# An attention output kept as hi and lo halves in DRAM, instead of split when it is read back

## What is computed

```python
x = x + attention(layernorm(x))        # 8 heads of 64; softmax(q k^T / 8) v, then @ W_out + b_out,
                                       # a layernorm with gamma, beta, (y + x_normalised) * 2**-0.5
x = x + mix(layernorm(x))              # token mixing with the previous token:
# r = sigmoid(xr @ W_r.T); k = relu(xk @ W_k.T)**2; out = r * (k @ W_v.T)
```

## Time and profile before

| what | value |
|---|---|
| median of 3 runs | 2963.3 us (2961.91 to 2963.69) |
| profiled execution, device time | 2955.59 us |
| its span, first to last instruction | 2953.8 us |
| attention pass | to about 2150 us |
| second pass | from 2154.3 us, a step each 47.6 us |
| TensorE busy | 2775.7 us (94%) |
| VectorE busy | 1795.2 us (61%) |
| ScalarE busy | 1223.7 us (41%) |
| GpSimd busy | 1342.6 us (45%) |
| mean granted TensorE clock | 0.972 of full speed |

### The profile page before, as it was taken

How to read it: one execution, slowest core, us unless ns; L and a number is a source line. 1 busy time by engine, 2 the same in 40 slices (tenths; PEclk the granted TensorE clock), 3 DMA queues, 4 the chain that set the end, 5 groups by cost and what they waited for, 6 DMA issues and landing times. The chain is left out here.

```text
span 2953.8 us, 37679 instructions
## 1 busy us (share of the span) xinstructions
PE 2775.7 (94%) x12400; PEld 1947.1 (66%) x12400; DVE 1795.2 (61%) x2888; ACT 1223.7 (41%) x1657; POOL 1342.6 (45%) x675
## 2 busy tenths in 40 slices
PE   5999999999999999999999999999959999999999
PEld 4666666566666656666665666666547777777777
DVE  5555455545645554664555456455368888888885
ACT  2334243334423432442343244233445655565554
POOL 2565355445535644563555365356613233332332
PEclk9999999999999999999999999999969999999999
DMA  3110111021111101111110111011031212111120
GB/s 100 54 26 22 52 29 26 18 55 29 26 47 27 29 22 52 31 24 50 23 33 22 48 29 29 15 29 54 22 100 58 71 57 71 60 67 67 61 71 29
DMA packets 72641, 128.39 MB, mean 43 GB/s; under 512 B 11024, under 2 KB 11536, under 8 KB 72464
## 3 DMA queue, kind: packets, MB, share of 16 engines
q1 hardware_dynamic: 72464, 126.14, 15.2%
HBM read 58.73 MB, written 33.55 MB: 31 GB/s over the span
## 5 line engine op out<-in xcount | busy, mean ns | idle before, releaser
L272 POOL TENSOR_TENSOR acc<-acc,probs 128x1024 f32<-128x1024 f32 x384 | 914.6, 2382 | 238.3 <-ACT probs L501 210.5
L354 DVE TENSOR_REDUCE half_max<-ps_max 128x1 f32<-128x512 f32 x1024 | 684.1, 687 | 524.8 <-PE ps_max L606 511.9
L501 ACT ACTIVATE probs<-ps_st 128x1024 f32<-128x1024 f32 x512 | 522.0, 1023 | 652.0 <-PE ps_st L626 633.0
L268 POOL TENSOR_TENSOR acc<-probs 128x1024 f32<-128x1024 f32 x64 | 152.9, 2389 | 786.9 <-ACT probs L501 786.9
L635 PE MATMUL ps_o<-probs,v 128*64 128x512 f32 x2048 | 468.5, 599 | 6.1 <-issue 6.1
L606 PE MATMUL ps_max<-kA,qA 128*128 128x512 f32 x1024 | 409.5, 428 | 30.8 <-DVE half_max L354 15.9
L625 PE MATMUL ps_st<-qA,kA 128*128 128x512 f32 x1024 | 424.3, 414 | 0.3 <-ACT probs L501 0.3
L626 PE MATMUL ps_st<-qB,kB 65*128 65x512 f32 x1024 | 412.7, 403 | 0.0
L635 PEld LDWEIGHTS ps_o<-probs,v 128*64 128x64 f32 x2048 | 136.1, 137 | 271.1 <-issue 240.2
L606 PEld LDWEIGHTS ps_max<-kA,qA 128*128 128x128 f32 x1024 | 194.4, 194 | 149.9 <-DVE half_max L354 49.5
L484 ACT ACTIVATE kA<-ps_misc,bqk 64x512 fp32r<-64x512 f32 x127 | 86.6, 682 | 430.1 <-PE ps_misc L569 427.3
(11 more groups left out here) (166 smaller groups left out, 4548.2 us busy)
## 6 DMA issues: line engine op xcount, KB each, us to landing
stage<-in_L_attn_x_dram SPq DMA_DIRECT2D x32, 512.0 KB, 5.8
qA<-qA SPq DMA_DIRECT2D x128, 128.0 KB, 2.2
kB<-kA SPq DMA_DIRECT2D x128, 128.0 KB, 2.3
o_scratch<-oT SPq DMA_DIRECT2D x128, 128.0 KB, 2.3
stage<-o_scratch SPq DMA_DIRECT2D x16, 1024.0 KB, 5.6
xc<-in_L_attn_x_dram SPq DMA_DIRECT2D x16, 1024.0 KB, 5.2
out_dram<-gate SPq DMA_DIRECT2D x64, 256.0 KB, 2.0
probs<-in_L_attn_W_qk_dram SPq DMA_DIRECT2D x4, 512.0 KB, 9.8
```

Source lines behind the costliest of these rows:

```text
L268: pool.tensor_tensor(acc[:, :], probs[:, 0, :], probs[:, 1, :], ALU.add).then_inc(acc_done, 1)
L272: pool.tensor_tensor(acc[:, :], acc[:, :], probs[:, j, :], ALU.add).then_inc(acc_done, 1)
L354: dve.tensor_reduce(half_max[:, r, kh:kh + 1], ps_max[(j + 1) % 2][:, :], AX_X, ALU.max).then_inc(max_done, 1)
L501: act.activation(probs[:, j, :], ps_st[j % 2][:, :], ACT.Exp).then_inc(exp_done, 1)
```

## The change

In the attention pass the output of each head is split where it is made. ScalarE copies oT to a new tile oT_hi (fp32r) after exponent j = 4 of the next head. VectorE subtracts, in place, oT - oT_hi after the row maximum j = 11. SP then issues four DMAs of 64x512 in place of two, into two DRAM arrays. oT_hi is single buffered, so its copy waits for the stores of the head before it. For the very last head both follow `normalise_o` at once.

In the second pass o_raw and both `split_o` are gone. SP loads o_hi and o_lo directly, 1 MB each in place of 1 MB in all, once the four y products of the chunk ahead are done. TensorE waits for the two loads. The load for chunk 0 is no longer made during the attention pass: it is the first thing that SP issues in the second one. SBUF holds one more tile of 128x512, DRAM one more array.

```diff
@@ attention pass, SP
                 def store_o(b, h):
-                    sp.wait_ge(o_done, 8 * b + h + 1)
+                    sp.wait_ge(oT_lo_done, 8 * b + h + 1)
                     for half in range(2):
-                        sp.dma_start(o_scratch[b][half, h, :, :],
-                                     oT[h % 2][half * DH:(half + 1) * DH, :]).then_inc(oT_free[h % 2], 16)
+                        dims = slice(half * DH, (half + 1) * DH)
+                        sp.dma_start(o_hi_scratch[b][half, h, :, :], f32(oT_hi[dims, :])).then_inc(oT_free[h % 2], 16)
+                        sp.dma_start(o_lo_scratch[b][half, h, :, :], oT[h % 2][dims, :]).then_inc(oT_free[h % 2], 16)
...
                         if h == 4 and last:
 
                             sp.wait_ge(xhat_done, 8 * B)
-                            for i in range(2):
-                                sp.wait_ge(oT_free[i], 16 + 128)
-                            sp.dma_start(stage[:, 0], chunks_of(o_scratch)[0]).then_inc(pass2_in, 16)
...
@@ attention pass, VectorE
+                def store_o_lo(b, h):
+
+                    dve.wait_ge(oT_hi_done, 8 * b + h + 1)
+                    dve.tensor_tensor(oT[h % 2][:, :].bitcast(F32R), oT[h % 2][:, :], f32(oT_hi[:, :]),
+                                      ALU.subtract).then_inc(oT_lo_done, 1)
...
                         for j in range(4, 16):
                             reduce_max(b, h + 1, j)
+                            if j == 11 and not first:
+                                store_o_lo(b, h - 1)
...
                         join_max(b, h + 1)
+                    else:
+                        store_o_lo(b, h - 1)
...
                 normalise_o(B - 1, HEADS - 1)
+                store_o_lo(B - 1, HEADS - 1)
...
@@ attention pass, ScalarE
+                def store_o_hi(b, h):
+
+                    act.wait_ge(o_done, 8 * b + h + 1)
+                    act.wait_ge(oT_free[(h - 1) % 2], 256 * b + 16 + 64 * ((h - 1) // 2 + 1))
+                    act.activation(oT_hi[:, :], oT[h % 2][:, :], ACT.Copy).then_inc(oT_hi_done, 1)
...
                         exponent(b, h, j, first)
+                        if j == 4 and not first:
+                            store_o_hi(b, h - 1)
...
                 store_inv(B - 1, HEADS - 1)
+                store_o_hi(B - 1, HEADS - 1)
...
@@ second pass, SP
                 def load_o(g):
-                    sp.dma_start(o_raw[:, :, :], o_view[g]).then_inc(o_in, 16)
+                    sp.dma_start(f32(o_hi[:, :, :]), o_hi_view[g]).then_inc(o_in, 16)
+                    sp.dma_start(f32(o_lo[:, :, :]), o_lo_view[g]).then_inc(o_in, 16)
...
+                load_o(0)
                 for dst, src in ((bo, b_out), (gam, gamma), (bet, beta)):
...
-                        sp.wait_ge(o_lo_done, g + 1)
+                        sp.wait_ge(y_done, 4 * g + 4)
                         load_o(g + 1)
...
@@ second pass, VectorE
-                def split_o(g):
-                    dve.wait_ge(o_hi_done, g + 1)
-                    dve.tensor_tensor(o_lo[:, :, :], o_raw[:, :, :], f32(o_hi[:, :, :]), ALU.subtract).then_inc(o_lo_done, 1)
...
-                    if more:
-                        split_o(g + 1)
...
@@ second pass, ScalarE
-                    if first and not (isinstance(g, int) and g == CHUNKS - 1):
-                        act.wait_ge(y_done, 4 * g + 4)
-                        split_o(g + 1)
...
@@ second pass, TensorE
-                        pe.wait_ge(o_hi_done, g + 1)
-                        pe.wait_ge(o_lo_done, g + 1)
+                        pe.wait_ge(o_in, 32 * g + 32)
```

More of the change, by code:

```diff
@@ L52, in rows_of, with attention_pass @@
     return 4 + (j - 8) // 2, j % 2
-def attention_pass(nc, x, w_qk, b_qk, w_v, b_v, w_out, w_r, w_out_raw, stage, o_scratch, ln1_stats, ident):
+def attention_pass(nc, x, w_qk, b_qk, w_v, b_v, w_out, w_r, w_out_raw, stage, o_hi_scratch, o_lo_scratch, ln1_stats, ident):
     with ExitStack() as ctx:
@@ L89, in attention_pass @@
         oT = [sb(f"oT{i}", [P, HALF]) for i in range(2)]
+        oT_hi = sb("oT_hi", [P, HALF], F32R)
         xb = stage[:, :, :, :].rearrange("p a k n -> p (a k) n")
@@ L162, in attention_pass @@
         o_done = sem("o_done")
+        oT_hi_done = sem("oT_hi_done")
+        oT_lo_done = sem("oT_lo_done")
         oT_free = [sem(f"oT_free{i}") for i in range(2)]
@@ L241, in _ @@
                 store_o(B - 1, HEADS - 1)
-                sp.wait_ge(pass2_in, 48)
+                sp.wait_ge(pass2_in, 32)
                 for i in range(2):
-                    sp.wait_ge(oT_free[i], 16 + 128 * B)
+                    sp.wait_ge(oT_free[i], 16 + 256 * B)
             @block.gpsimd
@@ L372, in normalise_o @@
                     dve.wait_ge(inv_stored, 8 * b + h + 1)
-                    dve.wait_ge(oT_free[h % 2], 128 * b + 16 + 32 * (h // 2))
+                    dve.wait_ge(oT_free[h % 2], 256 * b + 16 + 64 * (h // 2))
                     dve.tensor_tensor(oT[h % 2][:, :], ps_o[:, :], inv_cols[:, :], ALU.mult).then_inc(o_done, 1)
+                def store_o_lo(b, h):
+                    dve.wait_ge(oT_hi_done, 8 * b + h + 1)
+                    dve.tensor_tensor(oT[h % 2][:, :].bitcast(F32R), oT[h % 2][:, :], f32(oT_hi[:, :]),
+                                      ALU.subtract).then_inc(oT_lo_done, 1)
                 for t in range(TT):
@@ L830, in _, with mix_pass @@
                 spread_inv(B - 1, HEADS - 1)
-def mix_pass(nc, x, o_scratch, w_out_raw, stage, b_out, gamma, beta, w_k, w_v, mu_r, mu_k, out, ln1_stats, ident):
+def mix_pass(nc, x, o_hi_scratch, o_lo_scratch, w_out_raw, stage, b_out, gamma, beta, w_k, w_v, mu_r, mu_k, out, ln1_stats, ident):
     with ExitStack() as ctx:
@@ L858, in mix_pass @@
         xs = sb("xs", [P, NT, 2])
-        o_raw = stage[:, 0]
         o_hi = sb("o_hi", [P, KC, CHUNK], F32R)
@@ L900, in mix_pass @@
         x_in = sem("xc_in")
-        o_hi_done = sem("o_hi_done")
-        o_lo_done = sem("o_lo_done")
         y_done = sem("y_done")
@@ L935, in mix_pass @@
         out_done = sem("out_done")
-        o_view = chunks_of(o_scratch)
+        o_hi_view = chunks_of(o_hi_scratch)
+        o_lo_view = chunks_of(o_lo_scratch)
         x_view = x.rearrange("b (c t p) n -> (b c) p t n", c=2, p=P)
@@ L1090, in _ @@
                 residual_scales(0)
-                split_o(0)
                 dve.wait_ge(w_in["small"], 80)
@@ L1174, in weight_hi @@
                     act.activation(hi[n][:, kc, :], weight_bank(u), ACT.Copy).then_inc(w_hi_done, 1)
-                def split_o(g):
-                    if not (isinstance(g, int) and g == 0):
-                        act.wait_ge(o_in, 16 * g)
-                    act.activation(o_hi[:, :, :], o_raw[:, :, :], ACT.Copy).then_inc(o_hi_done, 1)
                 def mix_before(g, n, kc):
@@ L1327, in seq_preln_block @@
         w_out_raw = ctx.enter_context(nc.sbuf_tensor("w_out_raw", [P, KC, C], F32))
-        o_scratch = nc.dram_tensor("o_scratch", [B, 2, HEADS, DH, HALF], F32, kind="Internal").ap()
-        attention_pass(nc, x, w_qk, b_qk, w_v, b_v, w_out, w_r, w_out_raw, stage, o_scratch, ln1_stats, ident)
-        mix_pass(nc, x, o_scratch, w_out_raw, stage, b_out, gamma, beta, w_k, w_v2, mu_r, mu_k, out, ln1_stats, ident)
+        o_hi_scratch = nc.dram_tensor("o_hi_scratch", [B, 2, HEADS, DH, HALF], F32, kind="Internal").ap()
+        o_lo_scratch = nc.dram_tensor("o_lo_scratch", [B, 2, HEADS, DH, HALF], F32, kind="Internal").ap()
+        attention_pass(nc, x, w_qk, b_qk, w_v, b_v, w_out, w_r, w_out_raw, stage, o_hi_scratch, o_lo_scratch, ln1_stats, ident)
+        mix_pass(nc, x, o_hi_scratch, o_lo_scratch, w_out_raw, stage, b_out, gamma, beta, w_k, w_v2, mu_r, mu_k, out, ln1_stats, ident)
 _INS = ["L0_attn_x", "L0_attn_W_qk", "L0_attn_b_qk", "L0_attn_W_v", "L0_attn_b_v", "L0_attn_W_out", "L0_attn_b_out",
```

## The result

The changed kernel takes 3036.6 us (median of 4 runs, 3032.6 to 3039.4), the kernel before 2963.5 us on the same chip: a ratio of 1.0244, 95% interval 1.0226 to 1.0262. It is slower, by about twice the 34 us that were forecast. The profiled execution has a span of 3037.4 us, 83.6 us more than before, at a mean granted clock of 0.957 (before 0.972).

A forecast was written before the change was run, and what follows sets the result against it. TensorE was taken to bound both passes. Attention pass +51 us, between the passes +3.5 and second pass -20.7 gave +34 us, so 2997 us on the median of 2963.3; range 2972 to 3028 us.

The forecast's parts named there:

- TensorE sets the pace, VectorE's subtraction is held, 1.0 us a head: Attention pass: GpSimd's add holds the subtraction, delaying `rows` 14; 1.0 us a head, 1.4 in place 6, +51 us in all.
- Rival 2: Attention pass: the subtraction isn't held and fits the 1.2 us of room, leaving -17 us, 2946 us; chance 0.10.
- rival 3: Attention pass: the hold ends at the longest wait seen, +10 us in all, 2973 us; chance 0.06.
- The clock: Attention pass: granted clock 0.97 read as some 3% of the time at the lower level; nothing added for it.
- rival 4: Attention pass: added waits bring more low-clock time; with the push on GpSimd +75 us, 3038 us; chance 0.07.
- SP: "Nothing.": Attention pass: SP's two more issues a head (1.10 us) finish just when `copy_qk` becomes ready, so they cost nothing.
- in places 7 and 0: nothing: Attention pass, heads of places 7 and 0: GpSimd is idle at the subtraction and v products stand between, so no cost.
- The second pass: Removing the split shortens each step by 1.4 us, about 1.1 for step 0: -20.7 us; a `store_y` wait of about 0.5 stays.
- Rival 5: Second pass gains almost the whole 2 us a step, held wait as forecast: +25 us, inside the range; no chance given.
- Between the passes: From the last oT to the second pass's first matmul: copy, subtraction, more issues and two 1 MB loads add +3.5 us.

The follow-up runs named there:

- e9: The changed kernel, with SP issuing the next sequence's x loads ahead of the stores of place 7's head: 3024.6 us, ratio 1.0201 to the kernel before.
- e3: The changed kernel with a maximum over oT_hi (one SBUF input) in place of VectorE's subtraction: 2958.2 us, ratio 0.9966 to the kernel before.
- e5: The kernel before plus an idle VectorE maximum over 1888 columns behind row maximum 6 in places 1 to 5: ratio 1.0297.

## Why the prediction was wrong

**TensorE sets the pace, VectorE's subtraction is held, 1.0 us a head.** Right: 28.61 for 27.62 us, the wait of 40 us, the hold to the end of GpSimd's instruction plus 0.55 us. In place 6 all seven heads of the loop have a stretch; 35.4 less 1.55 is 33.85 for 32.3 us, 1.5 where 1.4 stood (three such heads of e9 have none and take 33.8). Rival 2, that it isn't held, and rival 3, that the hold ends sooner, are out: e3 and the 2.35 us show what they would have needed.

**The clock.** This step failed. The forecast took the lower clock as it was and made the waits' price their length; rival 4 named the mechanism, with 3038 us, and got 0.07. That its number lies so near the measured 3036.6 is partly luck: it also had GpSimd's late add delay `sum_rows`, which a head of 28.61 us leaves no room for, and it had no x loads. In the profiles the attention pass has 90 us more at the lower clock, and at 0.456 that is 41 of the 55 us that were missing in it. The runs scatter by some 10 us with the number of stretches, so a single profile sizes this badly: by the ratio (+72 us) less the direct +64 (40 in places 1 to 5, 12 in place 6, 12 in place 0) and the second pass's -23, it is 31 us. The profile of the kernel before is one with few stretches: 127 us up to the last oT, where the eight kernels without an added wait have 127 to 185, 158 in the middle; against 158 the 217 of after are 59 more, or 27 us. The earlier trace rows had shown 0.97, and the text took it for "some 3% of the time at the lower level". That level is 0.50 in the rows above, so it is 6% of the time: twice as many stretches as the text had in mind, and it didn't ask what decides whether a head gets one.

**SP: "Nothing."** This step failed too. The text asked whether `copy_qk` behind the stores would be late, and it hardly is (TensorE waits 6.0 us for it in the whole pass, 4.9 before). It didn't ask what else stands behind the last store of a sequence: the x loads, 20 us later than before, in the way of TensorE's loop end. Of "in places 7 and 0: nothing", the subtraction's own part is right (0.68 us but for one of 1.79, no wait behind it), but what it holds up on SP cost 12 us.

**The second pass: right in kind, too small.** 1.4 us a step was forecast and 2.0 measured (47.2 and 47.9 in turn to 45.50), 28.3 us for fourteen. The missing 0.6 us is a term left out: not only `mix(g, "k")` lost its hold, the four `mk_lo` did too (953 to 684 ns each in the mean, 1.1 us for four), because VectorE now comes to them without a break and GpSimd's add has to wait. So the wait for `store_y`, which the text kept at 0.5 us, went as well, and with no wait of TensorE left the gain is the most that the text's sum allowed (1.7 us and 0.3 us). That is read from the rows; no run has `mk_lo` held again. Rival 5 had that side. Against it stands that step 0 became 46.4 us, not 1.1 us shorter but 2.6 longer: TensorE waits 3.4 us once for `store_y` there.

**Between the passes** +3.6 us, forecast +3.5. Right; the second load took 7.8 us where 8 was put for it.

In sum, in the two profiled executions: attention +106 where +51 stood (clock +41, x loads +12, 2 us elsewhere), the rest -23 where -17 stood. By the ratio the attention pass is +95, with the clock at 31.

## What to carry to other kernels

An added wait on TensorE, where it bounds, may not be paid once: in this kernel, whose trace showed low-clock stretches already, it cost 1.5 to 2 times its length. Where a trace looks like this one, widen the range upwards. When an instruction gets a new wait, write down everything queued behind it in program order until the loop turns, the transfers of the next turn included, and look at what the DMA engines carry just where the bounding engine branches. A held instruction costs nothing where what stands behind it is needed only later: moving it by two reductions, with its stores in the next head, turned +2.4% into -0.4%, and giving the loads back their place made that -0.9%.

## What the runs showed that was not expected

- The hold works both ways. Back-to-back VectorE instructions with two SBUF inputs keep GpSimd out: two adds of 128x512, 1.29 us alone, took 5.19 us. The trace of before had it already: one such add of L1013 took 3.48 us.
- A reduction over one SBUF input ran its 0.68 us (512 columns) and 2.27 us (2048 columns) beside the same adds, with under 0.02 us of scatter.
- In places 1 to 5 low-clock stretches of 3.4 us at a granted clock of 0.50 come one to a head, 1.55 us each. Their number in 40 heads rose with the time that the wait added to a head: 10, 22, 30, 36 for 0, 0.45, 0.94 and 1.48 us, where kernels without an added wait scatter from 6 to 15. Why a wait of under 2 us brings more of them, and why in one head and not in the next of the same kind, stays open; e5 says only that the place of the wait doesn't decide it.
- Two transfers of 1 MB on one queue landed after 5.4 and 7.6 us, not one behind the other.
